# A block that hands its last stores on to the loads that read them, and a residual loaded earlier

## The reference

```python
def gat_layer(x, W, a_s, a_d, b, edge_index, concat):
    h = (x @ W).reshape(n, H, C)
    alpha_s = jnp.einsum('nhc,hc->nh', h, a_s)
    alpha_d = jnp.einsum('nhc,hc->nh', h, a_d)
    e = jax.nn.leaky_relu(alpha_s[src] + alpha_d[dst], NEG_SLOPE)
    ...
    return out + b
...
    x = _layernorm(x + _L0_gnn_ref(x, L0_gnn_W1, L0_gnn_a_src1, L0_gnn_a_dst1, L0_gnn_b1, L0_gnn_W2, L0_gnn_a_src2, L0_gnn_a_dst2, L0_gnn_b2, edge_index), axis=-1)
```

## Time and profile before

| | us |
|---|---|
| median of 3 runs | 1913.46 |
| lowest and highest of the 3 | 1913.06, 1915.37 |
| the profiled execution | 1919.87 |
| its span | 1918.1 |

### The profile page before, as it was taken

One profiled execution on the slowest core, in us unless ns is written; L12 is line 12 of the kernel. 1 busy time (PEld: TensorE's weight loads), 2 busy tenths in 40 slices (PEclk: granted clock), 3 DMA queues, 4 the chain that ended last, 5 costly groups with the idle time before them and its releaser, 6 DMA issues. The chain is left out here.

```text
span 1918.1 us, 26827 instructions
## 1 busy us (share of the span) xinstructions
PE 1794.1 (94%) x8951; PEld 1505.2 (78%) x8953; DVE 1242.8 (65%) x2171; ACT 711.9 (37%) x1149; POOL 691.5 (36%) x380
## 2 busy tenths in 40 slices
PE   8999799999999998896998998979999999999887
PEld 3444688998998998776986788867777888899876
DVE  9998687886887886664869866583224232453535
ACT  0203545444444443432466644222224233332221
POOL 1656231422422422211676764402323332323311
PEclk9999899999999999998999999989999999999899
DMA  1001640321321322103310031212222222323220
GB/s 20 14 8 60 229 157 28 113 67 51 116 67 51 116 67 99 50 25 121 119 50 1 10 104 60 75 71 71 66 81 86 86 86 63 101 80 103 82 103 33
DMA packets 54217, 143.38 MB, mean 75 GB/s; under 512 B 13780, under 2 KB 13908, under 8 KB 53076
## 3 DMA queue, kind: packets, MB, share of 16 engines
q1 hardware_dynamic: 47476, 109.01, 18.6%
q10 hardware_dynamic: 6624, 32.77, 4.7%
HBM read 129.18 MB, written 12.58 MB: 74 GB/s over the span
## 5 line engine op out<-in xcount | busy, mean ns | idle before, releaser
L752 POOL TENSOR_TENSOR w_pair<-early,w_pair 128x768 fp32r<-128x768 f32 x234 | 446.2, 1936 | 921.0 <-ACT w_pair L1370 920.8
L815 PE MATMUL ps<-w_pair,cols_x 128*128 128x384 f32 x2088 | 378.0, 338 | 5.6 <-issue 5.1
L815 PEld LDWEIGHTS ps<-w_pair,cols_x 128*128 128x128 f32 x2088 | 364.2, 189 | 11.8 <-issue 9.2
L815 PE MATMUL ps<-w_pair,wide 128*128 128x384 f32 x1872 | 336.3, 340 | 13.0 <-DVE wide L1765 11.7
L815 PEld LDWEIGHTS ps<-w_pair,wide 128*128 128x128 f32 x1872 | 331.9, 192 | 17.4 <-DVE wide L1765 12.9
L1370 ACT ACTIVATE w_pair<-early 128x768 fp32r<-128x768 f32 x234 | 181.2, 840 | 350.0 <-PE ps L815 157.1
L1316 PE MATMUL ps<-wide,w_pair 128*128 128x512 f32 x972 | 224.9, 391 | 2.2 <-DVE wide L1765 2.2
L1316 PEld LDWEIGHTS ps<-wide,w_pair 128*128 128x128 f32 x972 | 181.5, 188 | 39.8 <-DVE wide L1765 2.6
L428 PE MATMUL count_ps<-early,src_hot 128*128 (+1 forms) x814 | 178.8, 382 | 7.9 <-DVE early L348 7.7
L428 PEld LDWEIGHTS count_ps<-early,src_hot 128*128 (+1 forms) x816 | 80.2, 98 | 106.0 <-issue 8.8
L1284 PE MATMUL ps<-prob,wide 128*128 128x512 f32 x588 | 150.8, 396 | 0.0
(11 more groups left out here) (254 smaller groups left out, 2444.9 us busy)
## 6 DMA issues: line engine op xcount, KB each, us to landing
early<-weights SPq DMA_DIRECT2D x240, 384.0 KB, 3.1
edge_mask<-counts ACTq DMA_DIRECT2D x13, 512.0 KB, 3.3
multi<-attn ACTq DMA_DIRECT2D x8, 768.0 KB, 4.6
kept<-early ACTq DMA_DIRECT2D x3, 1536.0 KB, 6.0
multi<-kept ACTq DMA_DIRECT2D x3, 1536.0 KB, 6.5
counts<-out SPq DMA_DIRECT2D x8, 512.0 KB, 2.6
edge_mask<-masks ACTq DMA_DIRECT2D x5, 512.0 KB, 3.4
last_raw<-weights SPq DMA_DIRECT2D x6, 384.0 KB, 5.9
```

Source lines behind the costliest of these rows:

```text
L752: return nc.gpsimd.tensor_tensor(dst, whole, high.bitcast(F32), ALU.subtract)
L815: mm = nc.tensor.matmul(ps[:, m, 0:HW], left[:, a, k, m * P:(m + 1) * P], w_pair[:, slot_of[0], b, k, :], start=(k == 0 and a + b == 0), s ...
```

## The change

In the counting block, the store of mask 0 moves forward, ahead of the last two count matrices that SP stores; the store of the last count matrix goes from SP to ACT, whose copy of `rel_c` now stands ahead of its copy of `wkq`; masks 2, 1 and 3 follow the flag. SP waits for the older stores before the last three, and no longer for the last three, the flag and the last count matrix: these five add to `last_stored`, a semaphore that both blocks see, and the three count matrices before them to `stored`. In the layers block SP waits for these two ahead of the loads that read the stored data, and POOL waits for `last_stored` ahead of its first instruction. PE's reading of the flag and DVE's waits for the small loads move behind work that doesn't need them. At the second place the two loads go ahead of the copy of the weight columns, and the residual goes first.

```diff
-                sp.wait_ge(out16_ready, done + 1)
-                sp.dma_start(counts[slot], out16[:, half]).then_inc(pairs_stored if done < 4 else stored, 16)
-            for r, (ready, value) in enumerate(((mask_act, NB), (mask_dve, NB), (mask_act, 2 * NB), (mask_dve, 2 * NB))):
-                if r == 3:
-                    sp.wait_ge(flag_ready, 1)
-                    sp.dma_start(flag, flag_i[:]).then_inc(stored, 16)
+                if done == 5:
+                    sp.wait_ge(mask_act, NB)
+                    sp.dma_start(masks[0], mask[:, 0:NB]).then_inc(first_stored, 16)
+                if done < 7:
+                    sp.wait_ge(out16_ready, done + 1)
+                    sp.dma_start(counts[slot], out16[:, half]).then_inc(pairs_stored if done < 4 else stored, 16)
+            sp.wait_ge(flag_ready, 1)
+            sp.dma_start(flag, flag_i[:]).then_inc(last_stored, 16)
+            sp.wait_ge(hidden_in, 16 * 3)
+            sp.wait_ge(first_stored, 16)
+            sp.wait_ge(pairs_stored, 16 * 4)
+            for r, ready, value in ((2, mask_act, 2 * NB), (1, mask_dve, NB), (3, mask_dve, 2 * NB)):
                 sp.wait_ge(ready, value)
-                sp.dma_start(masks[r], mask[:, r * NB:(r + 1) * NB]).then_inc(stored, 16)
-            sp.wait_ge(hidden_in, 16 * 3)
-            sp.wait_ge(pairs_stored, 16 * 4)
-            sp.wait_ge(stored, 16 * (len(order) - 4 + 5))
+                sp.dma_start(masks[r], mask[:, r * NB:(r + 1) * NB]).then_inc(last_stored, 16)
...
+            act.wait_ge(c_ready, NB)
+            copy(out16[:, 2], rel_c[:]).then_inc(out16_ready, 1)
             act.wait_ge(wk_turned, 1)
             copy(wkq[:, :, 0, 0:8 * EARLY_R], ps[:, 0, 0, 0:8 * EARLY_R * KB].rearrange("p (k v) -> p k v", k=KB)).then_inc(wkq_hi, 1)
-            act.wait_ge(c_ready, NB)
-            copy(out16[:, 2], rel_c[:]).then_inc(out16_ready, 1)
+            act.wait_ge(out16_ready, 8)
+            act.dma_start(counts[SLOT3 + 2], out16[:, 2]).then_inc(last_stored, 16)
...
             sp.dma_start(b_cols[:], bias_cols).then_inc(small_in, 16)
+            sp.wait_ge(stored, 16 * 3)
+            sp.dma_start(vec, attn0[0:1].partition_broadcast(P)).then_inc(vec_in, 16)
+            sp.wait_ge(last_stored, 16 * 5)
             sp.dma_start(flag_sb[:], flag).then_inc(small_in, 16)
-            sp.dma_start(vec, attn0[0:1].partition_broadcast(P)).then_inc(vec_in, 16)
...
         def _(pool):
+            pool.wait_ge(last_stored, 16 * 5)
             nc.gpsimd.memset(ones_f, 1.0).then_inc(consts, 1)
...
             turn(0)
-            pe.wait_ge(small_in, 32)
-            many = pe.value_load(flag_sb[0:1, 0:1], min_val=0, max_val=1)
...
+            pe.wait_ge(small_in, 32)
+            many = pe.value_load(flag_sb[0:1, 0:1], min_val=0, max_val=1)
 
             def edge_sums(number, cnt, back=None, scaled=cols_done, first_back=0):
...
+            act.wait_ge(x_lo, 84)
+            act.dma_start(resid, x).then_inc(res_in, 16)
+            act.dma_start(b_row, bias_rows[0:1].partition_broadcast(P)).then_inc(b_in, 16)
             act.wait_ge(wk_turned, 2)
             last_cols = ps[:, 4, 0:8 * KB].rearrange("p (k v) -> p k v", k=KB)
             copy(wkq[:, :, 0, 8 * LAST_R:], last_cols).then_inc(wkq_ready, 1)
...
-            act.wait_ge(x_lo, 84)
-            act.dma_start(b_row, bias_rows[0:1].partition_broadcast(P)).then_inc(b_in, 16)
-            act.dma_start(resid, x).then_inc(res_in, 16)
             act.wait_ge(b_used, B_ROW_AT[0])
...
-            dve.wait_ge(small_in, 32)
-            dve.wait_ge(mask_in, 16)
-            dve.wait_ge(cnt_in, 16)
...
             source_columns(al[:, 0, 0], (ks[:, 0, 0], ks[:, 0, 1]))
+            dve.wait_ge(small_in, 32)
+            dve.wait_ge(mask_in, 16)
+            dve.wait_ge(cnt_in, 16)
             head(0, 0, 2, None, True, False)
```

14 lines of the change are left out of this document (9 added, 5 removed).

## The result

| | before | after |
|---|---|---|
| median of 8 runs each, us | 1914.58 (1912.43 to 1916.95) | 1907.68 (1903.50 to 1910.18) |
| the profiled execution, its span | 1919.87, 1918.1 | 1910.18, 1908.4 |

The ratio is 0.9961, with a 95% interval from 0.9950 to 0.9972: faster by 7.5 us (5.4 to 9.6). The sign was right, the size was not: the forecast was 1898.6, and 1907.68 lies above its range of 1894.5 to 1903.0. Two later measurements of the same kernel gave 0.9941 and 0.9953. The mean of the three is 0.9952, a gain of 9.2 us against a forecast of 14.9.

A forecast was written before the change was run, and what follows sets the result against it. It took TensorE (PE), busy 94% of the span, as the bound, so only its waits could yield gains: 4.9 us at the barrier plus 10.0 at the residual, 14.9 off the median 1913.46, gave 1898.6 us, range 1894.5 to 1903.0.

The forecast's parts named there:

- POOL's start, 214.0, and its gain of 4.8 us: At the barrier: POOL starts once the last stores have landed, at 214.0 in place of 218.82, 4.8 us earlier.
- the first gain: At the barrier, counted at the end of PE's first tile: 4.9 us, bounds 4.2 and 5.3.
- rival (b): Behind the barrier: the vectors' load delays the last stores up to 1.9 us; first gain 3.0, time 1900.5 us; chance 0.11.
- The first tile: PE's first 18 multiplies behind the barrier: end 5.3 us earlier, less 0.4 us for a lower clock.
- What comes next doesn't take it back.: Behind the first tile: PE works without a stop for 26 us, and the second pass's loads move by 4.8 us too.
- The residual's path: Second attention's end: residual issued at 857.15, landed by 865.8, additions start 8.5 us earlier, PE's stop shrinks to 2.3 us.
- The second gain, 10.0 us: At the residual: 10.0 us, between 8.5 with the clock as before and 11.3 where it stays up.
- From the span to the median: Whole kernel: the 14.9 us from the profiled execution hold for the median, 6.41 lower, since every execution has both waits.
- What is given back later: Behind both places: later stops move, and each low-clock stretch is worth up to 2.75 us, either way.
- (a): At the residual: clock stays low through most of the right half; second gain 8.5, time 1900.1 us; chance 0.15.
- (c): At the barrier: the block's end still waits for its stores; first gain 4.3, time 1899.2 us; chance 0.03.
- (d): First passes behind the barrier: PE works in pieces at the lower clock, up to 38 us lost, 1936.7 us; chance 0.02.

The follow-up runs named there:

- change_c: The change, unaltered, timed and traced a third time: 1906.48 us, ratio 0.9953 to the kernel before.
- pool_early: The change with POOL's wait for the last stores, constants and selection matrix moved behind the first pass's three low parts: 1904.40 us, ratio 0.9946.
- early_and_filled: The change with POOL's first three low parts ahead of its wait and PE's residual stop filled with 12 multiplies: 1904.43 us, ratio 0.9944.
- res_only: The kernel before with only the residual's two loads moved: 1911.37 us, ratio 0.9975.
- The part alone: The change without the residual's part, so only the barrier, the stores and the waits that take its place: 1912.19 us, ratio 0.9983.
- change_again: The change, unaltered, run once more for a second trace: 1903.92 us, ratio 0.9941 to the kernel before.
- filler: The change with 12 extra multiplies on PE in its 2.15 us stop at the residual: 1905.01 us, ratio 0.9945.

## Point by point: what the prediction had right and wrong

- **What bounds the kernel.** Right. Both waits were where it said, and both went. PE's total idle time fell by 12.6 us, past the 12 that it had set as a mark. But another of its signs of being wrong came true: a new wait for weights in the first pass, 2.71 us.
- **PE's start at the barrier**: 7.0 us earlier. Right in size: means over the traces 220.5 for the old block (five) and 213.8 for the change's three give 6.7, and 7.3 to 7.7 within a clock level, though the first pair of traces, of unlike levels, shows 4.99.
- **POOL's start, 214.0, and its gain of 4.8 us.** This is the step of the first gain that failed. POOL starts at 217.77, 217.81 and 218.55 in the change's three traces, and at 215.00 where the counting block's end kept its clock. Of the 1.0 us between 214.0 and 215.0, 0.4 is rival (b) in the one pair that prices it, and the rest a completion that took 0.9 us to arrive in place of 0.5 and small parts. The later starts come from the fall of the clock near 191, and in `change_c` 1.1 us more pass between PE's start and POOL's. The sum took the one trace that had no such fall as the rule; but that moves PE's start alike in both versions, and within a clock level POOL gains 3.8, 2.7 and 3.8 us in place of 4.8.
- **The first tile.** The 0.4 us for the lower clock in it measured 0.3 to 1.4 us (tile's end minus POOL's start, 7.06 and 1.1 us, in ten traces). With POOL's start this makes the gain at the tile's end 3.2, 2.3 and 3.8 us. The term was 4.9, its lower bound 4.2.
- **"What comes next doesn't take it back."** Right for the change: PE doesn't wait for DVE's scores (`kc`) in any of its three traces. The reason given was not enough, though. The row that was read as 26 us without a stop ended at 250 us with the view; the multiplies go on to 252.6, and a stop of 0.33 us for DVE's scores follows. That is what bounds any earlier start: in `pool_early` and `early_and_filled` PE starts its product 3 us earlier and waits 3.2 to 3.4 us there. In all, the first gain at Q is 294.1 (five traces, old block) minus 290.7 (three of the change), 3.4 us; counted without the two of `res_only`, 2.3. The part alone measured 3.3.
- **The residual's path.** Right in each step: issue at the end of DVE's probabilities, landing 6.6 us after it, additions without a wait, a stop of 2.15 us against 2.3 forecast, the 48 multiplies at 10.18 us between the 8.60 and 11.35 of its two ends. The Trainium skill (DMA: Bandwidth & Descriptors, "Anatomy of one DMA") gives the sum behind the estimate of 5.6 us for DMAs that GpSimd issues; this one is issued by ACT, and its 6.6 us are the measured number.
- **The second gain, 10.0 us.** Right against the trace that it was worked out from: 40.99 - 31.25 = 9.74. The term was mis-sized for the median: the same stretch takes 38.08 and 39.11 us in the other two traces of before, and 39.08 and 39.17 in those of the block part alone. With the mean of the three, 39.4, the gain at the place is 8.1. The lower clock had covered more of the right half's multiplies in the first trace than in the others (11.35 us for the 48; 10.66 and 9.97).
- **From the span to the median.** This step failed: "both places are waits that every execution has". They are, but their length is not the same in every execution. The three runs shown lay within 2.3 us of one another; the 24 later ones of the same kernel spread over 12 us, and the profiled one, 6.41 us above the first median, would be among their longest.
- **What is given back later.** The text allowed for it (each later stretch up to 2.75 us, either way), but gave the range only some 2 us for it above the other cases. From T1 to the end, the mean is 1023.6 us over three traces before and 1025.2 over three after: 1.6 us, in a quantity that scatters by 4.6 within one kernel.
- **The sum by the traces**, on means of three before and three after: 2.3 us up to Q, 1.0 from Q to R (559.4 and 558.3, in a stretch that scatters by 4), 8.1 at the residual, 1.6 back behind it, together 9.8, against 9.2 in the timed runs. Of the forecast's 14.9 that leaves 5.1 missing: 2.6 in the first gain, 1.9 in the second at its place and 1.6 behind it, less the 1.0 won between. The 7.5 us of the headline are the lowest of three measurements.
- **The rivals.** (a) is half true: the clock fell once in the right half, at 1.6 us of the 2.75. (b) is real, at 0.4 us in one pair and up to 1.5 across traces. (c) didn't happen: PE starts 3.9 us ahead of POOL. (d) is real in small: the tile runs at the lower level, but the clock is back at 225 to 227 us, and the passes up to the scores are not slow.

## What to carry to other kernels

A wait that ends is worth, at its place, what is late next, on every engine that meets there: here POOL, then DVE's scores, and PE's own chain was the wrong one to follow alone. A view that ends at 250 us can't show the stop at 252. Where single stretches depend on the clock, take the same stretch from several traces before pricing it, since one trace shows one draw; compare traces whose clock did the same before the place; and set a few named rows of all traces side by side before asking what a part has gained. For a difference of 10 us in 1900 measure three times: the same kernel gave 7.5, 11.3 and 9.0 us here.

## What the runs showed of the hardware

- The end of the program didn't follow small delays, and moved in steps. From the second attention's row sums to the end, 17 traces of ten kernels take 1054, 1058, 1061 or 1064 us, and in two traces of one kernel that differ by such a step the same 4771 multiplies are busy for 978.3 and 984.9 us. 1.7 us more work ahead of the turn left 1057.8 us, a value that the kernel has without it; 3.4 us more gave 1061.1.
- A stop of PE of 2.15 us cost 1.6 us in the multiplies behind it. Filling it with 12 idle multiplies got these back there, but the transposes behind took 1.3 us longer than in `change_again`, and from the row sums to the end the program took what one trace of the change takes without it (1054.5, 1054.3).
- Behind a stop of 2.63 us (`filler`) PE's product stood at 1.2 GHz until 224 us, 5.4 us long; without the stop (`pool_early`) it ran at 2.4 GHz from its start (granted clock 0.50 and 1.00).
- Loads issued right behind the last of four stores of 512 KB (27 KB and 768 KB) held back whoever waited for these stores, by 0.4 us in one pair of traces and by 0.3 to 1.5 us over nine against one. The first bytes of a store moved about 0.8 us behind its issue, and POOL went on 0.9 us behind the last of them.
